# Second cross-attention of a perceiver kernel: element ranks counted by TensorE in PSUM, one tile of projected keys, another order on ScalarE and VectorE

## The reference

```python
def _focus(x, focusing_factor):
    x = jnp.abs(jnp.where(x >= 0, x, LEAKY_SLOPE * x)) + EPS
    nrm = x.mean(axis=-1, keepdims=True)
    return jax.nn.softmax(jnp.log(x) * focusing_factor, axis=-1) * nrm
...
q = _focus(q @ Wq.T, focusing_factor); k = _focus(k @ Wk.T, focusing_factor); v = v @ Wv.T
qh, kh, vh = (_to_heads(q), _to_heads(k), _to_heads(v))
qh = _topk_sparsify(qh)
kh = _topk_sparsify(kh)
...
z_inv = jnp.einsum('bnd,bd->bn', qh, kh.mean(axis=1)) + EPS
kv = jnp.einsum('bnc,bnd->bcd', kh / sqrt_l, vh / sqrt_l)
y = jnp.einsum('bnc,bcd->bnd', qh, kv) / z_inv[..., None]
```

## Time and profile before

| | |
|---|---|
| median of 3 runs | 2884.91 us (2881.67 to 2885.43) |
| the profiled execution: its time, its span | 2881.91 us, 2879.8 us |
| busy in the span: PE, DVE, ACT, POOL | 85%, 79%, 64%, 29% |
| mean granted TensorE clock | 0.902 of 2.4 GHz |
| the second cross-attention's 19 steps | 2126.9 to 2453.2 us of the span |

### The profile page before, as it was taken

One profiled execution on the slowest core, in us unless ns is written; L12 is line 12 of the kernel. 1 busy time (PEld: TensorE's weight loads), 2 busy tenths in 40 slices (PEclk: granted clock), 3 DMA queues, 4 the chain that ended last, 5 costly groups with the idle time before them and its releaser, 6 DMA issues. The chain is left out here.

```text
span 2879.8 us, 34821 instructions
## 1 busy us (share of the span) xinstructions
PE 2444.1 (85%) x11795; PEld 1383.2 (48%) x11795; DVE 2272.1 (79%) x3112; ACT 1853.0 (64%) x2597; POOL 842.5 (29%) x470
## 2 busy tenths in 40 slices
PE   6899999997899999999999999996345666556997
PEld 3476666663344444444444444442134665354775
DVE  5687777764999999999999999994669998465454
ACT  5465555545788998889888888984334554213443
POOL 0122111101444444444444444441001000301554
PEclk9999999999899999999999999998556676656999
DMA  1000000001000000000000000000000010200211
GB/s 68 12 19 16 18 15 15 15 2 80 0 1 37 0 0 37 0 37 0 37 0 37 0 37 0 0 1 11 0 21 30 29 36 8 92 26 24 76 67 38
DMA packets 26069, 68.09 MB, mean 24 GB/s; under 512 B 3192, under 2 KB 15288, under 8 KB 24632
## 3 DMA queue, kind: packets, MB, share of 16 engines
q1 hardware_dynamic: 25632, 64.13, 6.5%
q10 hardware_dynamic: 288, 2.10, 0.2%
HBM read 60.91 MB, written 5.31 MB: 23 GB/s over the span
## 5 line engine op out<-in xcount | busy, mean ns | idle before, releaser
L251 PE MATMUL a_ps<-a_x,a_w 128*128 128x512 f32 x1536 | 695.4, 597 | 25.3 <-DVE a_kf L599 12.6
L251 PEld LDWEIGHTS a_ps<-a_x,a_w 128*128 128x128 f32 x1536 | 291.5, 191 | 404.6 <-issue 368.0
L774 POOL TENSOR_TENSOR a_den<-a_qf,a_ksum 128x1024 f32<-128x1024 f32 x128 | 271.0, 2117 | 510.7 <-DVE a_qf L592 474.1
L777 POOL TENSOR_TENSOR a_num<-a_qf,a_kvsum 128x1024 f32<-128x1024 f32 x128 | 294.8, 2303 | 186.1 <-DVE a_kvsum L617 186.0
L2425 DVE TENSOR_REDUCE x_rn<-x_sqk 128x8 f32<-128x512 f32 x256 | 174.3, 681 | 106.1 <-ACT x_sqk L2349 102.0
L2349 ACT ACTIVATE x_sqk<-x_b_k 128x512 f32<-128x512 f32 x256 | 152.9, 597 | 157.3 <-PE x_b_k L2261 151.0
L262 PE MATMUL a_ps<-a_att,a_w 128*128 128x512 f32 x480 | 215.8, 592 | 0.0
L592 DVE SCALAR_TENSOR_TENSOR a_qf<-a_eq,a_qf 128x1024 f32<-128x1024 f32 x128 | 195.3, 1526 | 1.7
L2242 POOL TENSOR_TENSOR x_kn<-x_craw,x_w 128x256 f32<-128x256 f32 x64 | 47.0, 734 | 503.3 <-DVE x_craw L2414 481.7
L445 ACT ACTIVATE a_den<-a_den,consts 128x1024 f32<-128x1024 f32 x128 | 147.0, 1148 | 55.8 <-POOL a_den L774 55.8
L599 DVE SCALAR_TENSOR_TENSOR a_kf<-a_ek,a_ps 128x1024 f32<-128x1024 f32 x128 | 155.5, 1215 | 28.2 <-ACT a_ps L441 20.9
(11 more groups left out here) (398 smaller groups left out, 5344.1 us busy)
## 6 DMA issues: line engine op xcount, KB each, us to landing
a_w<-layers SPq DMA_DIRECT2D x8, 2577.0 KB, 9.4
x_craw<-ctx SPq DMA_DIRECT2D x32, 256.0 KB, 2.7
y_cx<-ctx_t SPq DMA_DIRECT2D x16, 512.0 KB, 3.6
m_wb<-m_scratch SPq DMA_DIRECT2D x16, 512.0 KB, 3.8
m_w<-experts SPq DMA_DIRECT2D x8, 544.0 KB, 4.8
x_w<-xattn_w ACTq DMA_DIRECT2D x1, 1536.0 KB, 9.2
x_all<-x_t SPq DMA_DIRECT2D x4, 256.0 KB, 9.3
t_scratch<-t_q_t SPq DMA_DIRECT2D x4, 256.0 KB, 3.7
```

The lines of the kernel that those rows point to most:

```text
L251: last = nc.tensor.matmul(bank(tile, j), col(par, part * HK + u * P, P), x[:, t0:t0 + BANK], start=True, stop=True)
L774: nc.gpsimd.tensor_tensor(by_batch(den[:, b, :]), by_batch(qf[:, b, :]), bcast(ksum[:, b, :], S), ALU.mult).then_inc(d_ready, 1)
L777: nc.gpsimd.tensor_tensor(by_batch(num[:, b, :]), by_batch(qf[:, b, :]), bcast(kvsum[:, b, :], S), ALU.mult).then_inc(n_ready, 1)
```

## The change

- The two counts on VectorE and the subtraction go. VectorE only makes the seven comparisons, each into a tile of its own (`beats[d - 1]`), without waits between them.
- TensorE counts: `ranks` starts the PSUM tile `rank` with `later` (a constant: how many elements of the head come behind) times the identity `plus`, and adds for each d the comparison times `plus` to the columns from 16 d on and times `minus` (the identity negated) to the first ones. All operands are bf16, and each product is made for 4 groups at a time: 2 matmuls of 512 columns and 4 for each d, of 4 runs of 128 - 16 d columns.
- `select` (VectorE) reads the rank from PSUM. It waits for `ranked`, the last product.
- `rank` takes the PSUM tile of the second `k_tile`; `project_k(m)` now waits for `absolute(m - 1)` in place of `absolute(m - 2)`.
- TensorE's step: `project_k`, `outputs`, `ranks` 1 to 3, `project_v`, `ranks` 4 to 7, `sums`.
- ScalarE's step: `logs`, `negative`, `keep_values`, `invert_z`, `exponentials`; `negative` and `invert_z` stood behind `exponentials`. Ahead of step 0 `logs(0)` comes before `negative(1)`.
- VectorE's step: `mask_sums` before the first comparison, `minus_max` after the second, `divide` before `select`.

```diff
-        k_tile0, k_tile1, v_tile, kv = banks = [ctx.enter_context(nc.psum_tensor(f"y_ps{i}", [P, HALF], F32)) for i in range(4)]
-        k_tile = (k_tile0, k_tile1)
+        k_tile, rank, v_tile, kv = banks = [ctx.enter_context(nc.psum_tensor(f"y_ps{i}", [P, HALF], F32)) for i in range(4)]
...
-        beats = sb("beats", [P, 3, UT, P], BF16)
-        ahead = sb("ahead", [P, UT, P], BF16)
-        behind = sb("behind", [P, UT, P], BF16)
-        later = sb("later", [P, 1, P], BF16)
+        beats = [sb(f"beats{d}", [P, UT, P - d * XH1], BF16) for d in range(1, XDH1)]
+        later = sb("later", [P, UT // 2, P], BF16)
+        plus, minus = sb("plus", [P, P], BF16), sb("minus", [P, P], BF16)
...
-                    wait_past(pe, abs_done, m - 1)
+                    wait_past(pe, abs_done, m)
...
-                        last = nc.tensor.matmul(k_tile[b][0:rows_of(m), t * P:(t + 1) * P], tokens_of(m, t, b), w[:, c0:c0 + P],
+                        last = nc.tensor.matmul(k_tile[0:rows_of(m), t * P:(t + 1) * P], tokens_of(m, t, b), w[:, c0:c0 + P],
...
+                def ranks(n, links):
+                    r, c = rows_of(n), min(tiles_of(n), UT // 2)
+                    halves = tiles_of(n) // c
+                    view = rank[0:r, :].rearrange("p (t d) -> p t d", d=P)
+                    def add(weights, rhs, h, first, last, start=False, stop=False):
+                        return nc.tensor.matmul(view[:, c * h:c * (h + 1), first:last], weights[0:r, 0:r], rhs, start=start, stop=stop)
+                    if links[0] == 1:
+                        if not isinstance(n, int) or n > 0:
+                            pe.wait_ge(sel_done, n)
+                        for h in range(halves):
+                            add(plus, later[0:r, 0:c, :], h, 0, P, start=True)
+                    for d in links:
+                        pe.wait_ge(compared, n * (XDH1 - 1) + d)
+                        won = beats[d - 1]
+                        for weights, first, last in ((plus, d * XH1, P), (minus, 0, P - d * XH1)):
+                            for h in range(halves):
+                                done = add(weights, won[0:r, c * h:c * (h + 1), :], h, first, last,
+                                           stop=(d == XDH1 - 1 and weights is minus))
+                        if d == XDH1 - 1:
+                            done.then_inc(ranked, 1)
                 pe.wait_ge(w_loaded, 16)
                 project_k(0, 0, 0)
                 project_k(1, 1, 0)
+                pe.wait_ge(ranks_set, 1)
                 def step(n, b, i):
                     fixed = isinstance(n, int)
                     if not fixed or n + 2 <= LAST:
                         project_k(n + 2, b, i)
+                    if not fixed or n > FIRST:
+                        outputs(n - 1)
+                    ranks(n, (1, 2, 3))
                     if not fixed or 2 <= n + 1 <= LAST:
                         project_v(n + 1, 1 - b)
-                    if not fixed or n > FIRST:
-                        outputs(n - 1)
+                    ranks(n, (4, 5, 6, 7))
...
                 negative(0, 0)
+                logs(0, 0)
                 negative(1, 1)
-                logs(0, 0)
                 exponentials(0, 0)
                 def step(n, b, i):
                     fixed = isinstance(n, int)
                     if not fixed or n < LAST:
                         logs(n + 1, 1 - b)
+                    if not fixed or n + 2 <= LAST:
+                        negative(n + 2, b)
                     if not fixed or n >= 2:
                         keep_values(n, b)
+                    if not fixed or n > FIRST:
+                        invert_z(n - 1)
                     if not fixed or n < LAST:
                         exponentials(n + 1, 1 - b)
-                    if not fixed or n + 2 <= LAST:
-                        negative(n + 2, b)
-                    if not fixed or n > FIRST:
-                        invert_z(n - 1)
...
-                def choose(n, b, between):
-                    r, c = rows_of(n), tiles_of(n)
-                    v = (ex[:, b, :] if r == P else el[:, :]).rearrange("p (t d) -> p t d", d=P)
-                    up, down = ahead[0:r, 0:c, :], behind[0:r, 0:c, :]
-                    count = [LINKS * n]
-                    def first(d):
-                        return slice(0, P - d * XH1)
-                    def from_(d):
-                        return slice(d * XH1, P)
-                    def step(ins, back):
-                        ins.then_inc(chain, 1)
-                        count[0] = count[0] + 1
-                        dve.wait_ge(chain, count[0] - back)
-                    def compare(d, out, back):
-                        step(nc.vector.tensor_tensor(out, v[:, :, first(d)], v[:, :, from_(d)], ALU.is_ge), back)
-                    won = [beats[0:r, k, 0:c, :] for k in range(3)]
-                    compare(1, down[:, :, first(1)], 0)
-                    compare(2, won[2][:, :, first(2)], 1)
-                    step(nc.vector.tensor_tensor(up[:, :, from_(1)], down[:, :, first(1)],
-                                                 later[0:r, :, from_(1)].broadcast_to([r, c, P - XH1]), ALU.add), 1)
-                    for d in range(2, XDH1):
-                        k = d % 3
-                        if d + 1 < XDH1:
-                            compare(d + 1, won[(d + 1) % 3][:, :, first(d + 1)], 1)
-                        step(nc.vector.tensor_tensor(down[:, :, first(d)], down[:, :, first(d)], won[k][:, :, first(d)], ALU.add), 1)
-                        step(nc.vector.tensor_tensor(up[:, :, from_(d)], up[:, :, from_(d)], won[k][:, :, first(d)], ALU.add),
-                             1 if d + 1 < XDH1 else 0)
-                        if d == 3:
-                            between()
-                    step(nc.vector.tensor_tensor(won[0], up, down, ALU.subtract), 0)
-                    nc.vector.scalar_tensor_tensor(out=v, in0=won[0], scalar=float(KEEP), in1=v, op0=ALU.is_lt, op1=ALU.mult).then_inc(sel_done, 1)
+                def values_of(n, b):
+                    r = rows_of(n)
+                    return (ex[:, b, :] if r == P else el[:, :]).rearrange("p (t d) -> p t d", d=P)
+                def compare(n, b, links):
+                    r, v = rows_of(n), values_of(n, b)
+                    for d in links:
+                        nc.vector.tensor_tensor(beats[d - 1][0:r, 0:tiles_of(n), :], v[:, :, 0:P - d * XH1], v[:, :, d * XH1:P],
+                                                ALU.is_ge).then_inc(compared, 1)
+                def select(n, b):
+                    r, v = rows_of(n), values_of(n, b)
+                    dve.wait_ge(ranked, n + 1)
+                    nc.vector.scalar_tensor_tensor(out=v, in0=rank[0:r, 0:tiles_of(n) * P].rearrange("p (t d) -> p t d", d=P),
+                                                   scalar=float(KEEP), in1=v, op0=ALU.is_lt, op1=ALU.mult).then_inc(sel_done, 1)
...
-                for buffer, i in ((ahead, 0), (behind, XDH1 - 1)):
-                    nc.vector.memset(buffer[:, :, i * XH1:(i + 1) * XH1], float(XDH1 - 1 - i))
                 for i in range(XDH1):
-                    last = nc.vector.memset(later[:, :, i * XH1:(i + 1) * XH1], float(XDH1 - 1 - i))
-                last.then_inc(ranks_set, 1)
-                dve.wait_ge(ranks_set, 1)
+                    nc.vector.memset(later[:, :, i * XH1:(i + 1) * XH1], float(XDH1 - 1 - i))
+                nc.vector.tensor_copy(plus[:, :], ident)
+                nc.vector.tensor_scalar(minus[:, :], ident, -1.0, None, ALU.mult).then_inc(ranks_set, 1)
                 def step(n, b, i):
                     fixed = isinstance(n, int)
-                    def between():
-                        if not fixed or n > FIRST:
-                            mask_sums(n - 1)
-                        if not fixed or n < LAST:
-                            minus_max(n + 1, 1 - b)
                     if not fixed or n < LAST:
                         absolute(n + 1, 1 - b)
                     scales(n, b)
-                    choose(n, b, between)
+                    if not fixed or n > FIRST:
+                        mask_sums(n - 1)
+                    compare(n, b, (1, 2))
+                    if not fixed or n < LAST:
+                        minus_max(n + 1, 1 - b)
+                    compare(n, b, (3, 4, 5, 6, 7))
+                    if not fixed or n > FIRST:
+                        divide(n - 1)
+                    select(n, b)
                     if fixed and n < 2:
                         dve.wait_ge(sel_done, n + 1)
                         nc.vector.tensor_tensor(ex[:, b, :].rearrange("p (t d) -> p t d", d=P), ex[:, b, :].rearrange("p (t d) -> p t d", d=P),
                                                 bcast(scale[:, b, :], P), ALU.mult).then_inc(scaled, 1)
-                    if not fixed or n > FIRST:
-                        divide(n - 1)
```

(4 more changed lines are left out.)

9 lines of the change are left out of this document (4 added, 5 removed).

## The result

The changed kernel takes 2841.78 us (median of 4 runs, 2837.81 to 2843.15) against 2883.29 us (4 runs, 2880.33 to 2885.43) for the kernel before: ratio 0.9854, 95% interval 0.9837 to 0.9872. That is 41.5 us less. The profiled executions differ by 44.1 us, 2837.81 against 2881.91.

A forecast was written before the change was run, and what follows sets the result against it. VectorE was taken as the bound at 15.9 us a step, giving way to a 13.1 us chain. Steps 4 to 16 -36, tail -9, steps 0 to 3 -6: -51, so 2832 us, range 2820 to 2860.

The forecast's parts named there:

- VectorE loses 5 us a step and stops being the bound: Steps 4 to 16: VectorE sets the 15.9 us pace; additions and subtraction, 5.0 us a step, go, leaving 10.6.
- The new chain of a step at 2.4 GHz, 13.1 us: From one selection's end to the next, mostly TensorE work: 12.75 us, plus 0.35 for register work, is 13.1.
- The register work: Register operations ahead of the loop's seven waits, with its branch: 0 to 0.6 us a step, taken as 0.35.
- The counting takes 3.6 us: TensorE's new counting matmuls, 8192 columns of bf16 a step, take 3.6 us at 2.4 GHz.
- Side chains nearly tie and cost nothing: VectorE, the single k_tile, ScalarE and SyncE's context tile run beside TensorE's chain; no cost while TensorE is fast.
- So 2.4 GHz: TensorE in the new loop, 87% busy with one pause of 1.4 to 1.5 us a step, keeps the high clock.
- The second rival: Clock falls for 3 to 7 us in every second or third step: mean step 13.8 to 15.2, 2843 to 2862; chance 0.11.
- The tail, -9: Steps 17, 18 and the end together: 34.6 us against 43.5 before, so -9.
- Steps 0 to 3, -6: First steps, starting with an idle, slow TensorE: -6 us, between 0 and -12; step 2 gains nothing.
- Other five stages as before: The kernel's five other stages stay unchanged while this stage gets some 51 us shorter.

The follow-up runs named there:

- e6: Kernel before given the changed kernel's orders and its one tile of keys, VectorE still counting by additions and a subtraction: 2930.56 us.
- e8: Changed kernel plus 6 products that nobody reads on TensorE, ahead of the wait for the selection in sums: 2834.74 us.
- e3: Changed kernel with the counting products' outputs in one piece of PSUM instead of four runs: 2836.66 us.
- e4: Changed kernel with VectorE's mask_sums put back behind the third comparison: 2881.53 us.
- e2: Changed kernel with the wait for the selection in sums moved behind the two products of el and vlm: 2818.20 us.
- e5: Changed kernel with every order of the kernel before put back, as far as the counting allows: 2843.82 us.

## Why the prediction was right, and where it was not

The forecast was 2832 us in a range of 2820 to 2860; 2841.8 lies in it. The gain of 51 us was 41.5, or 44.1 between the profiled executions.

- *VectorE loses 5 us a step and stops being the bound*: right. Its busy time fell from 200.5 to 136.0 us, 4.96 a step. (The operations that go are 13 additions and the subtraction, one addition fewer than I counted: seven comparisons, 13 additions and one subtraction make 21 in `choose`, not 24. The 5 us came from distances between rows and don't change.) e6 shows the other side: with VectorE still counting, the same orders give 2930.56.
- *The new chain of a step at 2.4 GHz, 13.1 us*: right. A fast step is 13.07. By its terms: from the selection's end to sums 0.38 (I had 0.1), sums 2.95 (2.8), project_k 1.78 (1.8), outputs 1.12 (1.15), later to d = 3 2.53 (2.3), project_v 1.78 (1.8), d = 4 to 7 1.1 and depth 0.2 (1.55), selection 1.23 (1.2). The register work that I took at 0.35 shows partly: the pause before sums is 1.41 us in step 3 and 1.52 in the last three, which are written out, and 1.64 to 1.73 in the loop; e8 hides 0.2 of it.
- *The counting takes 3.6 us*: right, 3.5 without the wait at the third comparison (2.53 and 1.1 less some 0.1). The four runs cost nothing (e3). The Trainium skill, "PSUM — Partial Sum Buffer", section "Specifications (TRN2)", says that an access pattern that is not contiguous slows matmuls significantly; these rows don't agree, 0.54 us in both forms.
- *Side chains nearly tie and cost nothing*: right in a fast step, and the tie with VectorE is closer than I had it: the load of the weights for the third comparison's products waits up to 0.4 us, 4.6 us over 13 steps, of which some 0.1 us a step reaches the products. e4 and e2 show how near: 2.4 us more in a fast step with the mask late, 0.7 less with sums early.
- *"So 2.4 GHz"*: this is the step that failed, in part. The second rival, given 0.11, is what happens: 4 of 13 steps lose 1.6 us, 13 x (13.57 - 13.1) = 6 us. Its price was too high, 13.8 to 15.2 a step for 13.57; by its own terms, 1.5 to 3 us in every second or third step, it should have read 13.6 to 14.6. The rows I leaned on, the first stage with pauses of 1.89 and 1.72 us at clock 1.00, were true, and there are more of them:

```profile
45.77 1.06 PE L1871 MATMUL x_pa<-consts,x_qs 128*128 128x128 f32 x8 [1.34 <-ACT x_qn L1995]
50.26 1.06 PE L1871 MATMUL x_pa<-consts,x_qs 128*128 128x128 f32 x8 [1.31 <-ACT x_qn L1995]
54.48 1.06 PE L1871 MATMUL x_pa<-consts,x_qs 128*128 128x128 f32 x8 [1.43 <-ACT x_qn L1995]
```

Five pauses in a row, one in every 4.1 to 4.5 us, with TensorE busy 13.1 of the 19.5 us from 36.5 to 56, and the clock stays at 1.00. The new loop pauses once in 13.07 us, is busier (154.4 of 176.4 us), and loses it. So I carried one stage's behaviour over to another where neither the pause's length nor how often it comes foretells the clock; what does stays open. The Trainium skill, "TensorE: Matmul & The Clock Gate", section "HAM oscillation — how this bites in real kernels", has only pauses of some 3 us throw the clock back. Here one of 1.64 to 1.73 us does it in every third step; the trace doesn't agree.

- *The tail, -9*: -5, again the clock. Step 17 has slow sums (14.56 us from its first row to the next step's, against 12.8), step 18 takes 10.46 from selection to selection (10.4), and the projection out took 5.4 us at a clock of 0.68 where I had 3.6. With the clock held (e8) the tail is 34.8.
- *Steps 0 to 3, -6*: more, some 9 us: 67.4 against 76.4, and the entry comes 0.5 us later. Steps 0 and 1 gain 7.7 us together (21.35 against 29.00 from `absolute(1)` to `absolute(3)`), where I had 4 to 5; step 3 gains 1.8, step 2 nothing, as I had them. The block of GpSimd's product only moved, as said: five comparisons take 14.54 us.
- *Other five stages as before*: right, 426.6 us behind the stage in both.

In sum: -51 + 6 (steps) + 4 (tail) - 3 (start) = -44, as between the profiled executions; the other 2.6 us are between those and the medians. The mechanism of the gain is the forecast one. That the total is not further off is partly luck: the clock took back 10 us, and the start, for no reason that I had given, made up 3 of them.

## What to carry to other kernels

Where TensorE's work of a step ends in a result that another engine must read before the step can go on, as here, its chain has a pause in each step; work that doesn't need that result belongs there. It took 19.9 us off the stage at once (e2: 262.9 against 282.8); of the 1.21 us a step 0.7 are chain and 0.5 clock. Orders are worth something only as a set with the bound: the new orders cost 48.5 us without TensorE's counting (e6), gain 3.7 us of the stage with it (e5), and with VectorE's mask alone put back the whole gain was gone (e4).
